# Expert network: the last 128 tokens through all eight experts, 21 tiles in place of 23, a first load of one tile

## The chip, the cores and the metric

One core of one Trainium2 chip runs the whole network. The metric is device time of one execution in microseconds (us), lower is better. TensorE (PE) does products, VectorE (DVE) and ScalarE (ACT) do elementwise work, GpSimd (POOL) issues the indirect DMAs, SyncE (SP) the other DMAs. Numbers are f32 unless said otherwise.

## The reference

Sixteen layers run in a row, each on a layer norm of the running `x`, with its result added to it. The two expert networks (stages L2f and L2g) are:

```python
x = x + _L2_ffn_ref(_layernorm(x, axis=-1), ...)
...
    HIDDEN = 128; FFN = 4 * HIDDEN; NUM_EXPERTS = 8; TOP_K = 2
    xt = x.reshape(b * s, h)
    probs = jax.nn.softmax(xt @ gate_w + gate_b, axis=-1)
    _, idx = jax.lax.top_k(probs, TOP_K)
    one_hot = jax.nn.one_hot(idx, NUM_EXPERTS, dtype=xt.dtype)
    mask = (one_hot.sum(axis=1) > 0).astype(xt.dtype)
    h1 = jax.nn.relu(jnp.einsum('th,ehf->etf', xt, w1) + b1[:, None, :])
    out_e = jnp.einsum('etf,efh->eth', h1, w2) + b2[:, None, :]
    out = jnp.einsum('eth,te->th', out_e, mask)
```

Each token counts the results of its two best experts, unweighted. An expert is 128 -> 512 -> 128.

## The kernel before, in words

A loop over two passes runs all sixteen stages on two samples (1024 tokens, channels on the partitions), so each expert stage runs twice: four times in all. Within a stage the five engines run their own hand-written instruction streams, and semaphores tie them; the order below is the order in which the code is written, and no scheduler moves it.

`expert_ffn` (L432) works in these steps:

1. SP issues 16 loads of 256 KB of expert weights into `wall` (L500, L501) while the layer norm and the gate product run. DVE finds each token's two experts; PE counts and ranks them (L526 to L530); DVE lays the experts' rows out in 23 tiles of 128 slots (an expert begins a new tile) and writes each row's slot (L671).
2. PE turns the tokens to rows (L521), ACT copies them twice to `tok` (L594), and POOL scatters them to the slots in DRAM: 8 tiles of tokens, two picks each, 16 indirect DMAs (L742). Beside it PE turns the picks (L535, L536) and lays the second bias down in two accumulating banks (L542).
3. Once all scatters have landed (`sent`), SP loads the slots back in groups of four tiles (L505). PE turns a group (`turn`, L549), ACT copies it to `xt` (`x_copy`, L605).
4. The loop over 23 tiles: ACT copies the tile's expert out of `wall` into one of three `wsel` buffers (`choose`, L611; the expert's number is loaded from a tile first), PE makes the hidden products (L559), DVE adds the bias and takes the relu (L707), PE makes the result (L568), DVE copies it (L719), POOL scatters it to `rows` (L747).
5. SP loads `rows` back (L509), DVE adds each token's two rows (L723), PE turns the sums and adds them to the bias banks (L584), DVE adds those to `xs` (L726).

Of the kernel before, what the change touches and what calls it, by code (L numbers as in the profile page):

```python
# [5 lines left out]
P = 128  # L6
# [8 lines left out]
E = 8  # L15
# [5 lines left out]
SLOTS = (2 * NB * T + E * (P - 1)) // P  # L21
# [410 lines left out]
def expert_ffn(g, name):  # L432
# [5 lines left out]
    GROUP = 4  # L438
    with Stage(g, name) as st:
# [14 lines left out]
        place = st.sb("place", [P, NT, E])  # L454
        taken = st.sb("taken", [P, 2, NT, E])
        slot_f = st.sb("slot_f", [P, 2 * NT])
        slot = st.sb("slot", [P, 2 * NT], U32)
# [9 lines left out]
        tok = st.sb("tok", [P, 2, NT, WIDE])  # L467
        xg = st.sb("xg", [P, SLOTS, WIDE])
        xt = st.sb("xt", [P, 2, GROUP, P])
# [14 lines left out]
        expert_in, sent, x_turned, x_in = (st.sem(n) for n in ("expert_in", "sent", "x_turned", "x_in"))  # L484
        groups = -(-SLOTS // GROUP)
# [5 lines left out]
        size = lambda k: min(GROUP, SLOTS - GROUP * k)  # L491
        gate = g.ps[:, 0, 0:NT * E].rearrange("p (t e) -> p t e", e=E)
        counts = g.ps[:, 2, 0:NT * E].rearrange("p (t e) -> p t e", e=E)
        ranks = g.ps[:, 1, 0:NT * E].rearrange("p (t e) -> p t e", e=E)
        with g.nc.Block() as block:  # L495
            @block.sync
            def _(sp):
                st.clear_spent(sp)
                for e in range(E):
                    sp.dma_start(wall[:, e, 0:FF], g.experts[0, :, e * FF:(e + 1) * FF]).then_inc(expert_in, 16)  # L500
                    sp.dma_start(wall[:, e, FF:2 * FF], g.experts[1, :, e * FF:(e + 1) * FF]).then_inc(expert_in, 16)  # L501
                sp.wait_ge(sent, 16 * 2 * NT)
                for k in range(groups):
                    a, z = GROUP * k * P, (GROUP * k + size(k)) * P
                    sp.dma_start(xg[:, GROUP * k:GROUP * k + size(k), :], g.slots[a:z, :].rearrange("(t p) w -> p t w", p=P)).then_inc(group_in[k], 16)  # L505
                sp.wait_ge(returned, 16 * SLOTS)
                for b in range(NB):
                    rows = g.rows[2 * b * T:2 * (b + 1) * T, :].rearrange("(t p k) c -> p t k c", p=P, k=2)
                    sp.dma_start(back[:, b * KT:(b + 1) * KT, :, :], rows).then_inc(back_in[b], 16)  # L509

            @block.tensor
            def _(pe):
# [13 lines left out]
                pe.matmul(g.ps[:, 2, 0:NT * E], g.cb[:, ONES:ONES + P], flat, start=True, stop=True).then_inc(counted, 1)  # L526
                pe.wait_ge(tri_ready, 1)
                pe.matmul(g.ps[:, 1, 0:NT * E], below[:, :], flat, start=True, stop=False)
                for j in range(1, NT):
                    mm = pe.matmul(g.ps[:, 1, j * E:NT * E], g.cb[:, ONES:ONES + P], flat[:, 0:(NT - j) * E], start=False, stop=(j == NT - 1))  # L530
                mm.then_inc(ranked, 1)
                for b in range(NB):
                    for t in range(b * KT, (b + 1) * KT):
                        at = (t - b * KT) * P
                        pe.matmul(g.ps[0:E, 4 + b, at:at + P], picks_of[:, 0, t, :], g.w("ident"), start=True, stop=False)  # L535
                        mm = pe.matmul(g.ps[0:E, 4 + b, at:at + P], picks_of[:, 1, t, :], g.w("ident"), start=False, stop=True)  # L536
                    mm.then_inc(mask_turned, 1)
                pe.wait_ge(b2_in, 1)
# [5 lines left out]
                def turn(k):  # L544
# [3 lines left out]
                    for j in range(size(k)):  # L548
                        mm = pe.transpose(g.ps[:, 4 + k % 2, j * P:(j + 1) * P], xg[:, GROUP * k + j, 0:P], g.w("ident"))  # L549
                    mm.then_inc(x_turned, 1)  # L550

                def hidden_products(n):
                    pe.wait_ge(chosen, n + 1)
                    if n % GROUP == 0:
                        pe.wait_ge(x_in, n // GROUP + 1)
                    if n >= 2:
                        pe.wait_ge(relu, n - 1)
                    for f in range(FT):
                        mm = pe.matmul(g.ps[:, n % 2, f * P:(f + 1) * P], wsel[:, n % 3, f * P:(f + 1) * P],  # L559
                                       xt[:, n // GROUP % 2, n % GROUP, :], start=True, stop=True)  # L560
# [13 lines left out]
                for n in range(SLOTS):  # L574
                    if n % GROUP == 0 and n // GROUP + 1 < groups:
                        turn(n // GROUP + 1)
# [3 lines left out]
                for b in range(NB):  # L580
                    for t in range(b * KT, (b + 1) * KT):
                        at = (t - b * KT) * P
                        pe.wait_ge(summed, t // 2 + 1)
# [4 lines left out]
            def _(act):  # L588
                ln.scalar(act)
                for b in range(NB):  # L590
                    act.wait_ge(tok_turned, b + 1)
                    act.wait_ge(cleared, 1)
                    for k in range(2):
                        act.activation(tok[:, k, b * KT:(b + 1) * KT, 0:P], g.ps[:, 6 + b, :].rearrange("p (t c) -> p t c", c=P), ACT.Copy).then_inc(tok_in, 1)  # L594
                act.wait_ge(b2_turned, 1)
                act.activation(b2_t[:, :], g.ps[0:E, 3, 0:P], ACT.Copy).then_inc(b2_in, 1)
                for b in range(NB):
                    act.wait_ge(mask_turned, b + 1)
                    act.activation(mask_t[:, b * KT:(b + 1) * KT, :], g.ps[0:E, 4 + b, :].rearrange("e (t c) -> e t c", c=P), ACT.Copy).then_inc(mask_in, 1)

                def x_copy(k):
                    act.wait_ge(x_turned, k + 1)
                    if k >= 2:
                        act.wait_ge(hidden, GROUP * (k - 1))
# [2387 lines left out]
```

## Time and profile before

| | us |
|---|---|
| median of 3 runs (lowest to highest) | 2908.37 (2906.75 to 2912.24) |
| the profiled execution: its own time | 2909.99 |
| its span | 2908.4 |
| PE busy (12494 products) | 2280.9 (78%) |
| DVE / ACT / POOL busy | 1790.6 / 1394.1 / 863.1 |

The granted TensorE clock was 0.912 of full speed over the span. A share of busy time is a mean over sixteen unlike stages, so what a stage's edit is worth has to be read from that stage's own stretch. Times in rows are from the span's start.

### The profile page before, as it was taken

The numbers are of one execution on the slowest core, as the hardware profiler recorded it, in microseconds if no ns is written. First come the engines' busy times: TensorE is split into PE (matmuls) and PEld (weight loads), VectorE is DVE, ScalarE is ACT, GpSimd is POOL, SyncE is SP. The second block draws the span as 40 slices with busy tenths as digits, with TensorE's granted clock in tenths as the row PEclk, the third lists the DMA queues.
The fourth block names the chain that finished last, engine by engine and source line by source line (L and its number), as shares of the span: only waits on it lengthen the run. The fifth ranks groups of instructions, "written<-read, shape, count | busy, mean of one in ns | idle before, by whom it ended". The sixth has DMA issues, their size and how long they took to land. (4 is left out here: it accounts for less than half of the span.)

```text
span 2908.4 us, 36691 instructions
## 1 busy us (share of the span) xinstructions
PE 2280.9 (78%) x12494; PEld 1080.1 (37%) x12494; DVE 1790.6 (62%) x3175; ACT 1394.1 (48%) x2320; POOL 863.1 (30%) x854
## 2 busy tenths in 40 slices
PE   6678879999866757777766788799998668576777
PEld 2231244544355236223222222445443542352232
DVE  5958475555545725985559495655556456259865
ACT  5534626555432434645455355265554325346454
POOL 2822141000235333742037211510002343327420
PEclk8997999999978878999989989899999788789999
DMA  3002000000032131000000020000000321300000
GB/s 143 0 6 77 13 1 9 1 1 1 0 104 62 56 100 34 0 1 1 11 5 0 22 62 12 1 9 1 1 1 1 105 66 52 102 33 0 1 1 15
DMA packets 58913, 80.93 MB, mean 28 GB/s; under 512 B 10784, under 2 KB 38944, under 8 KB 58464
## 3 DMA queue, kind: packets, MB, share of 16 engines
q1 hardware_dynamic: 49376, 63.81, 6.8%
q0 software_dynamic: 4992, 10.76, 1.1%
q10 hardware_dynamic: 4352, 3.94, 0.5%
q8 instruction: 103, 1.69, 0.2%
q14 instruction: 90, 0.74, 0.1%
HBM read 53.83 MB, written 26.08 MB: 27 GB/s over the span
## 5 line engine op out<-in xcount | busy, mean ns | idle before, releaser
L2269 ACT ACTIVATE L1b_pr<-ps,L1b_mneg 128x512 f32<-128x512 f32 x256 | 173.8, 683 | 190.9 <-DVE L1b_mneg L2310 190.9
L2308 DVE TENSOR_REDUCE L1b_m<-ps 128x2 f32<-128x1024 f32 x128 | 156.7, 1225 | 88.7 <-PE ps L2159 82.9
L96 ACT ACT_TABLE_LOAD x44 | 56.5, 1283 | 283.0 <-PEq L495 66.2
L1520 POOL TENSOR_TENSOR L0a_db<-L0a_du,L0a_bs 128x1024 f32<-128x1024 f32 x64 | 150.5, 2360 | 105.2 <-DVE L0a_du L1631 59.6
L1520 POOL TENSOR_TENSOR L3a_db<-L3a_du,L3a_bs 128x1024 f32<-128x1024 f32 x64 | 150.5, 2360 | 104.1 <-DVE L3a_du L1631 57.6
L1943 ACT ACTIVATE L0b_pt<-ps 128x1024 f32<-128x1024 f32 x128 | 125.6, 1023 | 97.8 <-PE ps L1843 97.7
L2031 DVE TENSOR_REDUCE L0b_mx<-ps 128x1 f32<-128x512 f32 x256 | 157.8, 682 | 20.9 <-PE ps L1830 18.2
L267 POOL CAST L1g_xc<-xn 128x512 bf16<-128x512 f32 x2 | 1.5, 732 | 558.9 <-DVE xn L142 558.9
L2334 DVE COPY L1b_prt<-ps 128x512 f32<-128x512 f32 x128 | 88.5, 691 | 126.5 <-PE ps L2172 126.2
L1648 DVE TENSOR_TENSOR_SCAN L3a_hs<-ps,L3a_db 128x1024 f32<-128x1024 f32 x64 | 146.0, 2281 | 5.4 <-ACT ps L1440 5.4
L1648 DVE TENSOR_TENSOR_SCAN L0a_hs<-ps,L0a_db 128x1024 f32<-128x1024 f32 x64 | 146.0, 2281 | 4.6 <-ACT ps L1440 4.6
L2159 PE MATMUL ps<-L1b_k,L1b_q 64*128 64x512 f32 x512 | 144.5, 641 | 0.0
L1943 ACT ACTIVATE L2b_pt<-ps 128x1024 f32<-128x1024 f32 (+3 forms) x128 | 85.3, 706 | 114.8 <-PE ps L1843 114.0
L2184 PE MATMUL ps<-L1b_prt,L1b_v 128*64 128x512 f32 x512 | 136.7, 614 | 4.1 <-issue 2.0
L2172 PE MATMUL ps<-weights,L1b_pr 128*128 128x128 f32 x1024 | 135.3, 274 | 0.0
L2028 DVE CUSTOM_DVE_ANT_0 L2b_unmasked<-ps,weights 128x128 bf16<-128x128 f32 (+3 forms) x256 | 110.7, 487 | 36.0 <-PE ps L1830 33.0
L2172 PEld LDWEIGHTS ps<-weights,L1b_pr 128*128 128x128 f32 x1024 | 115.8, 140 | 45.5 <-issue 43.5
L1327 PE MATMUL ps<-L3a_hc,weights 128*128 128x512 f32 x256 | 127.4, 625 | 5.1 <-ACT L3a_du L1420 3.0
L1327 PE MATMUL ps<-L0a_hc,weights 128*128 128x512 f32 x256 | 125.0, 615 | 5.1 <-ACT L0a_du L1420 3.0
L121 PE MATMUL ps<-xs,weights 128*128 128x512 f32 x128 | 79.5, 754 | 53.2 <-issue 10.8
L1830 PE MATMUL ps<-L0b_ks,L0b_qs 64*128 64x512 bf16 x256 | 91.3, 446 | 28.9 <-DMA L0b_ks<-stack_dram 17.0
L2755 DVE TENSOR_SCALAR L3b_re<-L3b_qb,L3b_zk 128x512 f32<-128x512 f32 x192 | 88.4, 534 | 23.0 <-ACT L3b_qb L2593 10.8
(697 smaller groups left out, 5267.4 us busy)
## 6 DMA issues: line engine op xcount, KB each, us to landing
L2f_wall<-expert_dram SPq DMA_DIRECT2D x32, 256.0 KB
L2g_wall<-expert_dram SPq DMA_DIRECT2D x32, 256.0 KB
weights<-w_dram SPq DMA_DIRECT2D x5, 941.5 KB, 13.7
L0b_qs<-stack_dram SPq DMA_DIRECT2D x32, 96.0 KB, 2.2
stack_dram<-L0b_cut SPq DMA_DIRECT2D x24, 128.0 KB, 2.1
L2b_qs<-stack_dram SPq DMA_DIRECT2D x32, 96.0 KB, 2.3
stack_dram<-L2b_cut SPq DMA_DIRECT2D x24, 128.0 KB, 2.1
L2f_xg<-slots SPq DMA_DIRECT2D x10, 288.0 KB, 4.8
```

The source lines that it names most:

```text
L1327: mm = pe.matmul(g.ps[:, SUM + k, :], g.w("ident"), hc[:, n % DEEP, k, :], start=(s == 0), stop=(s == NS - 1))
L1520: pool.tensor_tensor(db[:, n % DEEP, :, :], du[:, b, :, :], bcast(bs[:, n % DEEP, :], 1, 2), ALU.mult).then_inc(input_ready, 1)
L1648: dve.tensor_tensor_scan(flat(hs), decay_banks(n).rearrange("p k t -> p (k t)"), flat(db), 0.0, ALU.mult, ALU.add).then_inc(scanned, 1)
L1830: pe.matmul(g.ps[:, bank, 0:span(t)], qs[r:r + HALF, b, 2 * i + c, t * P:(t + 1) * P], ks[r:r + HALF, b, 2 * i + c, 0:span(t)], start=True ...
L1943: act.activation(pt[:, n % 3, 2 * half:2 * half + 2, q0:T], g.ps[:, 2 * (s % 2):2 * (s % 2) + 2, q0:T], ACT.Exp).then_inc(prob, 1)
L2028: dve.tensor_tensor_reduce(unmasked[:, e % 3, 0:span(t)], g.ps[:, bank, 0:span(t)], g.w("causal_row", T - span(t)), 1.0, -3e38, ALU.add, A ...
L2031: dve.tensor_reduce(mx[:, u, col:col + 1], g.ps[:, bank, 0:T], AX.X, ALU.max).then_inc(top_in, 1)
L2159: mm = pe.matmul(g.ps[:, 2 * (s % 2) + h, :], q[HE * h:HE * h + HE, u % 3, t * P:(t + 1) * P], k[HE * h:HE * h + HE, u % 3, :], start=True ...
L2172: mm = pe.transpose(g.ps[:, 4 + h, j * P:(j + 1) * P], pr[:, s % 2, h, j * P:(j + 1) * P], g.w("ident"))
L2184: mm = pe.matmul(g.ps[HE * h:HE * h + HE, PV, :], v[:, u % 4, j, HE * h:HE * h + HE], prt[:, u % 2, h, j, :], start=(j == 0), stop=(j == K ...
L2269: act.activation(pr[:, s % 2, h, :], g.ps[:, 2 * (s % 2) + h, :], ACT.Exp, bias=mneg[:, s % 2, h:h + 1], accum_out=total[:, u % 2, t, h:h ...
L2308: dve.tensor_reduce(m[:, s % 2, :], g.ps[:, 2 * (s % 2):2 * (s % 2) + 2, :], AX.X, ALU.max).then_inc(max_raw, 1)
```

## The change

One tile of tokens, the last 128 of the second sample (`SENT = 7`), is no longer scattered. It goes through all eight experts straight from `xn` and `wall`: `full_hidden_products` and `full_results` on PE, `full_relus` on ACT, and on DVE a sum over the experts with the token's picks (`keep`) as factors, into the place that its turned sum takes (`both[:, SENT]`). The others need at most 21 tiles of slots. Groups of linear loads are 1, 2, 3, 4, 4, 4 and 3 tiles. The picks are turned after the eight experts; the weight loads have a semaphore each; ACT's `x_copy` of a group stands ahead of the `choose` beside it. Cut to its core (the wait on `full_sum` is in `turn`, the relus and the loop of copies are ACT's, and the last piece is DVE's, after its plan and ahead of its loop):

```diff
-SLOTS = (2 * NB * T + E * (P - 1)) // P
+SLOTS = (2 * (NB * T - P) + E * (P - 1)) // P
...
-    GROUP = 4
+    SENT = NT - 1
+    GROUPS = (1, 2, 3, 4, 4, 4, 3)
...
-                sp.wait_ge(sent, 16 * 2 * NT)
+                sp.wait_ge(sent, 16 * 2 * SENT)
...
                 mm.then_inc(gate_ready, 1)
-                for b in range(NB):
-                    for t in range(KT):
-                        mm = pe.transpose(g.ps[:, 6 + b, t * P:(t + 1) * P], g.xn[:, b, t * P:(t + 1) * P], g.w("ident"))
-                    mm.then_inc(tok_turned, 1)
-                pe.transpose(g.ps[0:E, 3, 0:P], g.w("e2_b2"), g.w("ident")).then_inc(b2_turned, 1)
+                pe.transpose(g.ps[0:E, 1, 0:P], g.w("e2_b2"), g.w("ident")).then_inc(b2_turned, 1)
+                for t in range(SENT):
...
+                def full_hidden_products(e):
+                    pe.wait_ge(expert_in[e], 32)
+                    if e >= 2:
+                        pe.wait_ge(full_relu, e - 1)
+                    for f in range(FT):
+                        mm = pe.matmul(g.ps[:, 2 + e % 2, f * P:(f + 1) * P], wall[:, e, f * P:(f + 1) * P], g.xn[:, 1, T - P:T], start=True, stop=True)
+                    mm.then_inc(full_hidden, 1)
+
+                def full_results(e):
+                    pe.wait_ge(full_relu, e + 1)
+                    for f in range(FT):
+                        mm = pe.matmul(g.ps[:, 4 + e // 4, e % 4 * P:(e % 4 + 1) * P], hd[:, e % 2, f, :], wall[:, e, FF + f * P:FF + (f + 1) * P],
+                                       start=(f == 0), stop=(f == FT - 1))
+                    mm.then_inc(full_out, 1)
+
+                full_hidden_products(0)
                 pe.wait_ge(mask_ready, 1)
...
                 mm.then_inc(ranked, 1)
+                for e in range(E):
+                    if e + 1 < E:
+                        full_hidden_products(e + 1)
+                    full_results(e)
+                pe.wait_ge(slots_ready, 1)
...
+                    else:
+                        pe.wait_ge(full_sum, E)
...
+                def full_relus(e):
+                    act.wait_ge(full_hidden, e + 1)
+                    if e >= 2:
+                        act.wait_ge(full_out, e - 1)
+                    if e == 0:
+                        act.wait_ge(ids, 2)
+                    for f in range(FT):
+                        ins = act.activation(hd[:, e % 2, f, :], g.ps[:, 2 + e % 2, f * P:(f + 1) * P], ACT.Relu, bias=wall[:, e, 2 * FF + f:2 * FF + f + 1])
+                    ins.then_inc(full_relu, 1)
+
+                take_tokens(0)
+                full_relus(0)
+                take_tokens(1)
+                for e in range(1, E):
+                    full_relus(e)
...
                 for n in range(SLOTS):
+                    if n == first_of[group_of[n]] and group_of[n] + 1 < groups:
+                        x_copy(group_of[n] + 1)
                     if n + 2 < SLOTS:
                         choose(n + 2)
-                    if n % GROUP == 0 and n // GROUP + 1 < groups:
-                        x_copy(n // GROUP + 1)
...
+                for e in range(E):
+                    dve.wait_ge(full_out, 4 * (e // 4) + 4)
+                    at = g.ps[:, 4 + e // 4, e % 4 * P:(e % 4 + 1) * P]
+                    if e == 0:
+                        dve.tensor_scalar(both[:, SENT, :], at, keep[:, 0:1], None, ALU.mult).then_inc(full_sum, 1)
+                    else:
+                        dve.wait_ge(full_sum, e)
+                        dve.scalar_tensor_tensor(out=both[:, SENT, :], in0=at, scalar=keep[:, e:e + 1], in1=both[:, SENT, :],
+                                                 op0=ALU.mult, op1=ALU.add).then_inc(full_sum, 1)
```

On PE, at the gate product of L2f, the order before; `L2f_mask` is the count of the picks:

```order
L517 MATMUL ps<-weights,xn 128x8 x8
L521 MATMUL ps<-weights,xn 128x128 x8
L523 MATMUL ps<-weights 8x128
L526 MATMUL ps<-L2f_mask,cb 128x64
L528 MATMUL ps<-L2f_mask,L2f_below 128x64
```

Now the first expert's hidden products stand ahead of the count:

```order
L525 MATMUL ps<-weights,xn 128x8 x8
L527 MATMUL ps<-weights 8x128
L530 MATMUL ps<-weights,xn 128x128 x7
L539 MATMUL ps<-xn,L2f_wall 128x128 x4
L552 MATMUL ps<-L2f_mask,cb 128x56
L555 MATMUL ps<-L2f_mask,L2f_below 128x56
```

The count waits behind four products that weren't there. On PE, from the bias product (L542, now L573) to the first results of the loop, before:

```order
L542 MATMUL ps<-L2f_mask_t,L2f_b_t 128x512 x2
L549 MATMUL ps<-weights,L2f_xg 128x128 x4
L559 MATMUL ps<-L2f_xt,L2f_wsel 128x128 x4
L549 MATMUL ps<-weights,L2f_xg 128x128 x4
L559 MATMUL ps<-L2f_xt,L2f_wsel 128x128 x4
L568 MATMUL ps<-L2f_wsel,L2f_h 128x128 x4
```

The same place now:

```order
L573 MATMUL ps<-L2f_mask_t,L2f_b_t 128x512 x2
L582 MATMUL ps<-weights,L2f_xg 128x128
L593 MATMUL ps<-L2f_xt,L2f_wsel 128x128 x4
L582 MATMUL ps<-weights,L2f_xg 128x128 x2
L593 MATMUL ps<-L2f_xt,L2f_wsel 128x128 x4
L602 MATMUL ps<-L2f_wsel,L2f_h 128x128 x4
```

One turned tile stands ahead of the first products, and the second products now belong to the group turned just ahead of them. On ACT, at the opening of the loop (the third choice of an expert), before:

```order
L605 ACTIVATE L2f_xt<-ps 128x512
L610 TENSOR_LOAD L2f_expert_of
L610 ISA x2
L611 ISA
L611 ACTIVATE L2f_wsel<-L2f_wall 128x1028
L605 ACTIVATE L2f_xt<-ps 128x512
```

The same place now:

```order
L657 ACTIVATE L2f_xt<-ps 128x128
L657 ACTIVATE L2f_xt<-ps 128x256
L662 TENSOR_LOAD L2f_expert_of
L662 ISA x2
L663 ISA
L663 ACTIVATE L2f_wsel<-L2f_wall 128x1028
L657 ACTIVATE L2f_xt<-ps 128x384
```

Each group's copy has moved ahead of the choice that it stood behind.

## Rows read from the trace of the kernel before

**Rows 1.** Windows: the first L2f in two stretches, then both passes of L2g.

```profile
core 0: us, PE busy (x) PEld busy (x) DVE busy (x) ACT busy (x) POOL busy (x), PEclk, DMA share, GB/s
826.31:847.84 21.53, 5.12 (x23) 2.69 (x21) 1.84 (x9) 3.18 (x4) 15.60 (x16) 0.58 0.17 56
852.85:900.17 47.32, 46.66 (x387) 45.21 (x387) 31.65 (x125) 24.59 (x26) 20.73 (x22) 0.97 0.14 43
1036.70:1139.54 102.84, 69.70 (x485) 60.41 (x485) 43.89 (x169) 35.66 (x43) 38.33 (x44) 0.78 0.29 95
...
2487.56:2590.00 102.44, 69.52 (x485) 60.36 (x485) 43.56 (x169) 35.66 (x43) 38.34 (x44) 0.78 0.29 95
```

**Rows 2.** Timeline of L2f, scatters to first products: start, length, engine, line, idle before.

```profile
827.82 0.96 POOL L742 DMA_INDIRECT slots<-L2f_tok,L2f_slot  x1 [0.31 <-issue]
...
845.52 0.96 POOL L742 DMA_INDIRECT slots<-L2f_tok,L2f_slot  x1 [0.30 <-issue]
847.84 3.34 SPq L505 DMA_DIRECT2D L2f_xg<-slots  x6
...
850.95 1.12 PE L549 MATMUL ps<-weights,L2f_xg 128*128 128x128 f32 x4 [19.52 <-DMA L2f_xg<-slots]
...
852.10 0.60 ACT L605 ACTIVATE L2f_xt<-ps 128x512 f32<-128x512 f32 x1 [19.28 <-PE ps L549]
852.74 1.06 ACT L611 ACTIVATE L2f_wsel<-L2f_wall 128x1028 f32 x1
...
852.85 2.04 PE L559 MATMUL ps<-L2f_xt,L2f_wsel 128*128 128x128 f32 x8 [0.78 <-ACT L2f_xt L605]
```

**Rows 3.** Timeline of the loop of L2f, from one group's turn to the next.

```profile
863.10 0.60 PE L549 MATMUL ps<-weights,L2f_xg 128*128 128x128 f32 x4
...
863.93 1.06 ACT L611 ACTIVATE L2f_wsel<-L2f_wall 128x1028 f32 x1 [0.73 <-PE ps L568]
864.43 1.06 PE L568 MATMUL ps<-L2f_wsel,L2f_h 128*128 128x128 f32 x8
...
865.33 1.06 PE L559 MATMUL ps<-L2f_xt,L2f_wsel 128*128 128x128 f32 x8
...
870.95 0.60 PE L549 MATMUL ps<-weights,L2f_xg 128*128 128x128 f32 x4
```

**Rows 4.** DMA issues: size of one in KB, median us from issue to landing.

```profile
L0b_qs<-stack_dram SPq DMA_DIRECT2D x32, 96.0 KB, 2.2
```

**Rows 5.** Timeline of L2f: PE around the count, the turned picks and the bias.

```profile
821.09 0.42 PE L523 MATMUL ps<-weights 128*8 128x128 f32 x1
...
822.90 0.24 PE L526 MATMUL ps<-L2f_mask,cb 128*128 128x64 bf16 x1 [1.40 <-DVE L2f_mask L650]
...
828.93 0.38 PE L535 MATMUL ps<-weights,L2f_picks_of 128*8 128x128 f32 x2
...
829.14 0.38 PE L536 MATMUL ps<-weights,L2f_picks_of 128*8 128x128 f32 x2
...
829.46 1.98 PE L542 MATMUL ps<-L2f_mask_t,L2f_b_t 8*128 8x512 f32 x4
```

**Rows 6.** Windows of half a microsecond around the changes of the granted clock.

```profile
828.50:829.00 0.50, 0.50 (x6) 0.39 (x5) 0.00 (x0) 0.00 (x0) 0.28 (x1) 0.94 0.00 0
...
832.00:832.50 0.50, 0.00 (x0) 0.00 (x0) 0.00 (x0) 0.50 (x1) 0.50 (x1) 0.50 0.07 19
...
1058.50:1059.00 0.50, 0.00 (x0) 0.00 (x0) 0.00 (x0) 0.00 (x0) 0.20 (x2) 1.00 0.00 0
...
855.50:856.00 0.50, 0.50 (x5) 0.50 (x4) 0.50 (x3) 0.22 (x1) 0.00 (x0) 0.64 0.04 12
```

**Rows 7.** Lines L861 and L881: copies and sums out of PSUM, min/median/max in ns.

```profile
L861 ACT ACTIVATE L2a_prt<-ps x16: 277/438/599, 794.8 to 2261.0; 128x128 f32<-128x128 f32 x4, 128x256 f32<-128x256 f32 x4, 128x384 f32<-128x384 f32 x4, 128x512 f32<-128x512 f32 x4
...
L881 DVE SCALAR_TENSOR_TENSOR L2a_none<-ps,L2a_later x16: 283/482/692, 790.7 to 2258.1; 128x128 f32<-128x128 f32 x4, 128x256 f32<-128x256 f32 x4, 128x384 f32<-128x384 f32 x4, 128x512 f32<-128x512 f32 x4
```

**Rows 8.** Timeline of L2f's end: the sums of the rows loaded back.

```profile
909.34 0.76 DVE L723 TENSOR_TENSOR L2f_both<-L2f_back 128x256 f32<-128x256 f32 x2 [0.61 <-DMA L2f_back<-rows]
```

More of the change, by code:

```diff
@@ L437, in expert_ffn @@
     NT = NB * KT
-    GROUP = 4
+    SENT = NT - 1
+    GROUPS = (1, 2, 3, 4, 4, 4, 3)
+    first_of = [sum(GROUPS[:k]) for k in range(len(GROUPS) + 1)]
+    group_of = [k for k in range(len(GROUPS)) for _ in range(GROUPS[k])]
     with Stage(g, name) as st:
@@ L453, in expert_ffn @@
         limit = st.sb("limit", [P, E])
[L454 to L457, printed above, removed]
+        place = st.sb("place", [P, SENT, E])
+        taken = st.sb("taken", [P, 2, SENT, E])
+        slot_f = st.sb("slot_f", [P, 2 * SENT])
+        slot = st.sb("slot", [P, 2 * SENT], U32)
+        keep = st.sb("keep", [P, E])
+        hd = st.sb("hd", [P, 2, FT, P])
         past = st.sb("past", [P, SLOTS, E])
@@ L529, in _ @@
-                for j in range(1, NT):
-                    mm = pe.matmul(g.ps[:, 1, j * E:NT * E], g.cb[:, ONES:ONES + P], flat[:, 0:(NT - j) * E], start=False, stop=(j == NT - 1))
+                pe.wait_ge(b2_in, 1)
+                pe.matmul(g.ps[:, 1, 0:SENT * E], below[:, :], flat[:, 0:SENT * E], start=True, stop=False)
+                for j in range(1, SENT):
+                    mm = pe.matmul(g.ps[:, 1, j * E:SENT * E], g.cb[:, ONES:ONES + P], flat[:, 0:(SENT - j) * E], start=False, stop=(j == SENT - 1))
@@ L547, in turn @@
                         pe.wait_ge(x_in, k - 1)
-                    for j in range(size(k)):
-                        mm = pe.transpose(g.ps[:, 4 + k % 2, j * P:(j + 1) * P], xg[:, GROUP * k + j, 0:P], g.w("ident"))
+                    else:
+                        pe.wait_ge(full_sum, E)
+                    for j in range(GROUPS[k]):
+                        mm = pe.transpose(g.ps[:, 4 + k % 2, j * P:(j + 1) * P], xg[:, first_of[k] + j, 0:P], g.w("ident"))
                     mm.then_inc(x_turned, 1)
@@ L574, in _ @@
                 for n in range(SLOTS):
[L575 to L576 removed]
+                    if n == first_of[group_of[n]] and group_of[n] + 1 < groups:
+                        turn(group_of[n] + 1)
                     if n + 1 < SLOTS:
@@ L650, in _ @@
                 dve.tensor_tensor(mask[:, :, :], picks_of[:, 0, :, :], picks_of[:, 1, :, :], ALU.add).then_inc(mask_ready, 1)
+                dve.tensor_tensor(keep[:, :], picks_of[:, 0, SENT, :], picks_of[:, 1, SENT, :], ALU.add).then_inc(keep_ready, 1)
                 dve.wait_ge(counted, 1)
@@ L713, in _ @@
                 for n in range(SLOTS):
-                    if n % GROUP == 1 and n // GROUP + 1 < groups:
-                        rows_of(n // GROUP + 1)
+                    if n + 1 == first_of[group_of[n] + 1] and group_of[n] + 1 < groups:
+                        rows_of(group_of[n] + 1)
                     if n + 1 < SLOTS:
@@ L721, in _ @@
                     dve.wait_ge(back_in[b], 16)
-                    for t in range(b * KT, (b + 1) * KT, 2):
-                        dve.tensor_tensor(both[:, t:t + 2, :], back[:, t:t + 2, 0, :], back[:, t:t + 2, 1, :], ALU.add).then_inc(summed, 1)
+                    for t in range(b * KT, min(SENT, (b + 1) * KT), 2):
+                        z = min(SENT, t + 2)
+                        dve.tensor_tensor(both[:, t:z, :], back[:, t:z, 0, :], back[:, t:z, 1, :], ALU.add).then_inc(summed, 1)
                 for b in range(NB):
```

92 lines of the change are left out of this document (49 added, 43 removed).

## The prediction

> **What bounds the kernel now.** I read first how much time the edited stage holds. An L2g takes 102.8 and 102.4 us in the two passes, and the L2f's look the same, so four such stages hold some 410 of the 2908 us [rows 1]. Nothing outside them is edited. Then I read the first L2f by stretches. From 826.31 to 847.84 POOL is the only busy engine worth the name (15.60 of 21.53 us, PE 5.12): the stage waits for 16 scatters, issued one after the other. From 852.85 to 900.17 PE is busy 46.66 of 47.32 us: the loop over 23 tiles is bound by PE [rows 1]. The timeline shows the seam between the two: the last scatter is issued at 845.52, the first linear load at 847.84, its data lets PE start at 850.95 after 19.52 us of idling, and the first products start at 852.85, once four tiles are turned and copied [rows 2]. All of this is serial, so what leaves it leaves the stage. The idle PE in the scatters' stretch is the room into which the change puts the eight experts.
>
> **The change, term by term, for one stage.** Negative is time saved.
>
> A. Two scatters go. From 827.82 to 845.52 lie 14 pitches, 1.264 us each [rows 2]; two are -2.53.
>
> B. The first load holds 72 KB (128 rows of 144 numbers) and not 288. The trace has no load of this size on this path. The old one takes 850.95 - 847.84 = 3.11 us [rows 2], which is the upper end (no gain); the nearest small one, 96 KB, lands in 2.2 [rows 4]. Ends 0 and -0.9; I take -0.8, since the size is nearer to the small row.
>
> C. One tile is turned and copied ahead of the first products. Now that takes 852.85 - 850.95 = 1.90 [rows 2]. One of four transposes is 1.12/4 = 0.28, a copy of 128x128 out of PSUM 0.28 [rows 7], and the two gaps seen between turn, copy and products are 0.03 and 0.15 [rows 2]: 0.74, so -1.15.
>
> D. Two tiles of the loop go. A group of four, its turn included, takes 870.95 - 863.10 = 7.85, so 1.96 a tile [rows 3]: -3.92.
>
> E. The second tile's products now need the copy of the group turned just ahead of them, where they used to run from the first group. PE idles for the drain of the transposes, the copy of two tiles (0.28 for one, 0.44 as the median of one to four tiles [rows 7]) and the gap of 0.15: +0.75. Between 0.6 and 0.9.
>
> F. The copy stands ahead of the choice beside it. In rows 3 the choice starts at 863.93 and the products that need it at 865.33. If the copy goes first it starts at 863.74, after the turn, takes 0.60 [rows 2], and the choice (1.06) ends near 865.45 to 865.55, some 0.1 to 0.25 late. The load of the expert's number does not add to this: behind a copy that had not waited for the loop, the choice followed at 852.74, 0.04 after the copy's end [rows 2]. Six openings, minus what the same move gives back (choice n+3 is then no longer late): +0.5, between 0 and 1.5.
>
> G. TensorE's clock. PE starts at half rate after its idle time, and the row in which the rate rises is 855.50 to 856.00 (0.64 granted), 4.7 us after the first transpose [rows 2, 6]. If PE idles again before the loop, this repeats; but less of it is spent on turn and copy (0.9 instead of 1.9 us), so about 1 us more of products runs at half: +0.5.
>
> H. The count of the picks waits behind the first expert's hidden products. PE is free at 821.51 and the count starts at 822.90 after 1.40 idle [rows 5]. Eight passes at half rate take 2 x 0.90 = 1.8 (the pitch of a set of eight at full rate is 865.33 - 864.43 = 0.90 [rows 3]), less one transpose that is gone, so the scatters start about 0.2 later in L2f; in L2g the clock is still up there and it fits. Mean +0.1, between 0 and 0.5.
>
> I. The second load of returned rows is a quarter smaller, and its last sum half as long; DVE waits 0.61 us for it [rows 8]: -0.3.
>
> The slots' arithmetic on DVE gets a few columns narrower and `keep` fits in DVE's wait for the count: 0. Thirteen more semaphores are cleared by SP at the start of the next stage, ahead of any DMA that is due: 0.
>
> Sum: -2.53 - 0.8 - 1.15 - 3.92 + 0.75 + 0.5 + 0.5 + 0.1 - 0.3 = -6.85. Four stages: -27.4.
>
> **What has to stay hidden.** The added work costs nothing only if PE and ACT are done when the first tile lands, at 850.95 - 2.53 - 0.8 = 847.6. PE has the counts behind it at about 823.5. Then follow 15 sets of eight passes (7 hidden, 8 results), 0.90 each at full rate, 1.8 at half. In the trace of before, PE starts again at 822.90 and has the full rate at 828.50 to 829.00 (0.94) [rows 5, 6]. Taken so, 2.8 sets run by 828.5 and the other 12.2 end at 839.5. The 16 products that turn the picks come 0.21 apart (828.93, 829.14 [rows 5]): 842.9. Bias products 1.98: 844.9. ACT needs four relus an expert, near 0.28 each [rows 7], 1.1 us against PE's 1.8, so PE sets the pace; ACT's second copy of the picks ends at 843.6 and its first two choices at 846.2. DVE's eight sums at about 0.3 [rows 7] end by 842. So PE has 2.7 us to spare and ACT 1.4. The group turned at the start finds both.
>
> **A rule on the clock.** What the rows show is mixed. PE's idle time after the bias products brought the clock to 0.50 by 832.00 in L2f, while in L2g it was still 1.00 in the window 1058.50 to 1059.00 with PE idle [rows 6]. The Trainium skill (TensorE: Matmul & The Clock Gate, "HAM oscillation — how this bites in real kernels") says that waits for a DMA that are long enough throttle PE, so that each burst opens cold, while shorter ones leave it warm. By that rule the loop could open at full rate in this kernel. I make of it the first rival; what it would give is worked out from rows alone.
>
> **Rivals.**
>
> 1. The clock stays up into the loop. PE would idle 844.9 to 847.6, 2.7 us, where it idled 19.52. Then the 3.8 us of products at half rate (4.7 less 0.9) shrink to half and the first transpose too: -2.0 more, -8.85 a stage, 2909.99 - 35.4 = 2874.6. For it speaks the window at 1058.50; against it the one at 832.00.
>
> 2. The loads and openings give less. The first load lands no sooner (B = 0) and each of six openings costs 0.25 (F = 1.5): -5.05 a stage, 2889.8. For it: the six loads go out within 3.34 us and share the engines; the small row is of another transfer. Against: a first load has nothing ahead of it in its queue.
>
> 3. The eight experts outlast the scatters, on the other side. If the clock does not rise during them, the 12.2 sets take 11.0 more and the turned picks 3.4 more, and PE is done at 859.3, 11.7 after the first tile. The stage ends 11.7 - 6.85 = 4.9 later than before: 2909.99 + 19.4 = 2929. It decides from 2.7 us on, that is when three more sets run at half rate, or when an expert's four relus take over 2.1 us. Against it: before, PE reached the full rate with less to do in the same place, and held it through the loop with the same sets of eight (0.97 granted over 852.85 to 900.17 [rows 1]).
>
> **How the numbers follow.** The profiled execution took 2909.99, 1.6 above the median of 2908.37 and inside the three runs' spread, so I take the sum against it: 2909.99 - 27.4 = 2882.6. Chances: forecast 0.60, with its own range 2877 to 2888; rival 1 0.18 (in some of the four stages it would lie between the two); rival 2 0.13; rival 3 0.09, a part of it only slightly late and near no change. The range 2871 to 2895 holds the first three with some margin and leaves out rival 3. A measurement of this kernel tells about 0.2% (5.8 us) from no change: faster by more 0.89, within it 0.02, slower 0.09.
>
> **What would show it.** Right: 14 scatters at 1.26 and 21 at the end; first linear load 2.3 us after its issue; PE in sets of eight from about 823 on, the clock at full rate by 829, the bias products over before the first transpose; the first products near 848.3 on the old scale; groups of four at 7.9 to 8.1 us. Wrong: a first transpose whose wait ends with the bias products or DVE's sum (rival 3); a PE clock of 1.00 in the first microseconds of the loop (rival 1); waits for `wsel` over 0.25 at each opening, or 3 us for the small load (rival 2). If the scatters' pitch grew beside a busy PE, ACT and DVE, term A would be wrong, since this pitch was seen beside idle engines only.

## The result, and the profile after

The changed kernel takes 2927.86 us in the median of five runs (2926.85 to 2942.85), the one before 2908.37 (2905.77 to 2912.24): ratio 1.0073, 95% interval 1.0058 to 1.0089. It is slower, where 2882.6 was forecast.

The profiled execution of after is the slowest of its five: 2942.85 us, span 2941.2. So I compare the edited stages, from the count of the picks to the last sum. The windows of both L2g stages, from there (columns: length, busy time and instructions of PE, PEld, DVE, ACT, POOL, granted clock, DMA share, GB/s):

```profile
1054.23:1150.30 96.07, 75.43 (x537) 69.88 (x537) 39.68 (x155) 35.40 (x61) 33.65 (x35) 0.84 0.21 67
2524.98:2618.08 93.10, 71.48 (x537) 66.14 (x537) 39.69 (x155) 34.94 (x59) 33.57 (x35) 0.86 0.22 69
```

Before, the same stretches take 90.41 (1049.13 to 1139.54, the end as in [rows 1]) and 90.45. Over all four stages after is 17.1 us longer; the other 15.7 of the 32.8 between the two spans lie in stages that nothing edited. That unedited rest takes 2546 us in the profiled execution of before, 2562 in that of after, and 2535 to 2564 over the profiled executions of all kernels here. The medians are 19.5 apart. Below are the means of the four stages, in us, with those of the experiments that follow. A stage is cut at the first product of the count of the picks, the first transpose of a loaded tile, the first products of the loop, the loop's last result and the last sum into `xs`:

| kernel | count to first transpose | to first products | to last result | to last sum | stage |
|---|---|---|---|---|---|
| before | 27.73 | 1.87 | 48.22 | 12.68 | 90.5 |
| after | 34.86 | 1.21 | 46.38 | 12.33 | 94.8 |
| no experts | 24.02 | 0.90 | 46.82 | 12.25 | 84.0 |
| groups only | 26.63 | 0.91 | 51.25 | 12.40 | 91.2 |
| all scatters paced | 30.92 | 0.91 | 47.00 | 12.21 | 91.0 |
| eight paced | 27.79 | 0.91 | 47.18 | 12.27 | 88.2 |
| scatters held | 36.49 | 0.90 | 47.34 | 12.34 | 97.1 |
| split | 27.83 | 0.89 | 46.87 | 11.96 | 87.6 |
| split, no sum wait | 26.70 | 0.91 | 47.24 | 11.97 | 86.8 |
| split, choice first | 27.29 | 0.91 | 46.00 | 11.97 | 86.2 |
| choice first, picks last | 26.47 | 0.90 | 46.06 | 11.97 | 85.4 |
| choice first, L2g paced | 25.46 | 0.90 | 46.13 | 11.97 | 84.5 |

All that after loses, it loses between the count and the first transpose. There the timeline of its first L2f has, on POOL and SP, what was forecast: scatters 1.26 apart, two fewer of them, and the loads behind them (against [rows 2]):

```profile
842.51 0.96 POOL L805 DMA_INDIRECT slots<-L2f_tok,L2f_slot  x1 [0.30 <-issue]
843.78 0.96 POOL L805 DMA_INDIRECT slots<-L2f_tok,L2f_slot  x1 [0.30 <-issue]
845.05 0.96 POOL L805 DMA_INDIRECT slots<-L2f_tok,L2f_slot  x1 [0.30 <-issue]
847.35 3.50 SPq L512 DMA_DIRECT2D L2f_xg<-slots  x7
```

The first tile's load has a median of 1.9 us to landing, so it lands near 849.3. But PE isn't ready. Its sets of eight in the same stretch (L539 hidden products, L545 results):

```profile
831.37 1.06 PE L539 MATMUL ps<-xn,L2f_wall 128*128 128x128 f32 x8
832.27 1.06 PE L545 MATMUL ps<-L2f_wall,L2f_hd 128*128 128x128 f32 x8
833.16 1.06 PE L539 MATMUL ps<-xn,L2f_wall 128*128 128x128 f32 x8
835.38 1.16 PE L545 MATMUL ps<-L2f_wall,L2f_hd 128*128 128x128 f32 x8 [1.16 <-issue]
836.38 1.06 PE L539 MATMUL ps<-xn,L2f_wall 128*128 128x128 f32 x8
844.02 2.08 PE L545 MATMUL ps<-L2f_wall,L2f_hd 128*128 128x128 f32 x8 [6.59 <-ACT L2f_hd L641]
845.89 1.62 PE L539 MATMUL ps<-xn,L2f_wall 128*128 128x128 f32 x8
849.83 3.21 PE L545 MATMUL ps<-L2f_wall,L2f_hd 128*128 128x128 f32 x16 [2.31 <-ACT L2f_hd L641]
...
856.99 1.98 PE L573 MATMUL ps<-L2f_mask_t,L2f_b_t 8*128 8x512 f32 x4
858.90 0.34 PE L582 MATMUL ps<-weights,L2f_xg 128*128 128x128 f32 x1
```

And ScalarE's relus between them:

```profile
828.89 1.14 ACT L641 ACTIVATE L2f_hd<-ps,L2f_wall 128x128 f32<-128x128 f32 x4 [0.65 <-PE ps L539]
830.68 1.14 ACT L641 ACTIVATE L2f_hd<-ps,L2f_wall 128x128 f32<-128x128 f32 x4 [0.65 <-PE ps L539]
834.19 1.14 ACT L641 ACTIVATE L2f_hd<-ps,L2f_wall 128x128 f32<-128x128 f32 x4 [2.36 <-remote]
842.83 1.14 ACT L641 ACTIVATE L2f_hd<-ps,L2f_wall 128x128 f32<-128x128 f32 x4 [7.50 <-remote]
848.63 2.17 ACT L641 ACTIVATE L2f_hd<-ps,L2f_wall 128x128 f32<-128x128 f32 x8 [4.67 <-PE ps L539]
```

To the fourth relu all is as reckoned: sets 0.90 apart, a relu every 1.79. The next ones start long after the products that they need. The relu of 842.83 needs the set that starts at 833.16 and is done by 834.2, and a buffer that the results of 832.27 had read; ACT was free at 835.33. It waits 7.5 us, and the trace can name no instruction that ended it: `remote` stands where a signal comes so long after every instruction that could have sent it that none is named. The first of the two experts at 848.63 needs a set that ended at 837.44 (836.38 and 1.06). ACT's own signals are prompt: PE's results start at 844.02, 0.05 after the relus end. So what is late is TensorE's signal to another engine. The packed trace has the signals' own times, and they say it outright: those of the eight sets of hidden products come 0.01, 0.01, 0.01, 0.01, 1.73, 8.59, 11.18 and 1.28 us after the sets' modelled ends. Some arrive while scatters are still issued (834.16, 842.80), others together some 2.6 us after the last one (848.5 to 848.8). In the list of waits nothing of `remote` stood in the kernel before; now (total us, times, longest):

```profile
ACT L2g_hd L641 <- remote: 25.6, 4, 10.3
DVE L2g_both L751 <- remote: 23.5, 2, 15.3
ACT L2f_hd L641 <- remote: 21.5, 3, 11.6
```

The length of a wait is not the delay. DVE's 15.3 us began while the results that it needs were still being made; they ended at 1064.20, 10.6 us before it starts:

```profile
1063.04 1.16 PE L545 MATMUL ps<-L2g_wall,L2g_hd 128*128 128x128 f32 x8
1074.84 0.35 DVE L751 TENSOR_SCALAR L2g_both<-ps,L2g_keep 128x128 f32<-128x128 f32 x1 [15.30 <-remote]
```

The longest delay of a signal in after is 13.9 us (second pass of L2f: a set's end at 2298.71, its signal at 2312.61).

The Trainium skill (Perfetto Trace Analysis, "Tensor Engine Instruction (MATMUL, LD_WEIGHTS)") warns of this gap: a matmul's end in the trace is computed, while the semaphore goes out once PSUM has acknowledged the data and becomes visible later still. The rows agree that a signal can come after the end shown, and put the gap at up to 13.9 us, where the Trainium skill gives no size. They don't tell which of its steps took the time.

### The profile page after: what moved, and what is told of

Same layout as the page of the kernel before. It is cut to its first block and busy times, and to the rows that moved or that the text cites. A ratio compares the mean times of both kernels' runs of the same rounds, so it can differ in the third digit from the quotient of the medians.

```text
span 2941.2 us, 37607 instructions
## 1 busy us (share of the span) xinstructions
PE 2346.3 (80%) x12842; PEld 1141.0 (39%) x12862; DVE 1790.7 (61%) x3179; ACT 1421.7 (48%) x2444; POOL 847.0 (29%) x838
## 5 line engine op out<-in xcount | busy, mean ns | idle before, releaser
L2006 ACT ACTIVATE L0b_pt<-ps 128x1024 f32<-128x1024 f32 x128 | 125.6, 1023 | 97.1 <-PE ps L1906 97.0
L1390 PE MATMUL ps<-L3a_hc,weights 128*128 128x512 f32 x256 | 123.3, 608 | 5.1 <-ACT L3a_du L1483 3.0
L1390 PE MATMUL ps<-L0a_hc,weights 128*128 128x512 f32 x256 | 122.6, 605 | 5.1 <-ACT L0a_du L1483 3.0
L121 PE MATMUL ps<-xs,weights 128*128 128x512 f32 x128 | 81.8, 773 | 52.5 <-issue 10.1
```

What stands on the lines that cost most here:

```text
L1390: mm = pe.matmul(g.ps[:, SUM + k, :], g.w("ident"), hc[:, n % DEEP, k, :], start=(s == 0), stop=(s == NS - 1))
L2006: act.activation(pt[:, n % 3, 2 * half:2 * half + 2, q0:T], g.ps[:, 2 * (s % 2):2 * (s % 2) + 2, q0:T], ACT.Exp).then_inc(prob, 1)
```

## Experiments

The edits are shown cut to their core. There were two theories at the start. S: TensorE's signals reach the other engines late while GpSimd issues scatters back to back. R: the experts' own chain is slower than I reckoned, scatters or not.

**No experts.** From after, the experts' products, relus and sums are left out (the last tile gets zeros):

```diff
-                full_hidden_products(0)
-                for e in range(E): ...            # PE, ACT and DVE alike
+                dve.tensor_scalar(both[:, SENT, :], g.w("ident"), 0.0, None, ALU.mult)
```

> This leaves the last tile's way through the experts out: no products, relus and sums of it (zeros stand for its result), all else as in the changed kernel (14 scatters, 21 tiles, groups of 1, 2, 3, 4, 4, 4, 3). Theory S (TensorE's signals reach the other engines late while GpSimd issues scatters back to back, which holds up the eight experts) and theory R (the eight experts' own work is slower than I had it) both expect what my terms A to I gave without the experts: 2878 to 2888 us. If the time is over 2895, the saving of 27 us was wrong in itself, and the experts are the smaller part of the miss.

2888.86 us (2885.83 to 2891.04), ratio to before 0.9935 (0.9915 to 0.9955). The median lies 0.9 us above my range. The stages lose 6.5 us each against -6.95, which is my sum without H (this kernel has no hidden products ahead of the count): the terms hold, and what is wrong is the cover.

**Scatters held.** From after:

```diff
                 pool.wait_ge(slots_ready, 1)
+                pool.wait_ge(full_out, E)
```

> GpSimd starts the 14 scatters only when all eight experts' results are there. Theory S: with no scatter beside them the signals are prompt, a set of eight passes takes 0.9 us and the eight experts end about 12 to 14 us after the counts (at 838 to 840 in the first L2f); the scatters come after, and the whole is within 10 us of the changed kernel (2925 to 2940). Theory R: the experts keep their pace of the changed kernel (end at 853), the scatters come on top, +15 us a stage: 2980 to 2990.

2953.24 us, ratio 1.0158 (1.0134 to 1.0182), between the ranges, but the trace decides. With no scatter beside them the last relus stand

```profile
834.90 1.14 ACT L641 ACTIVATE L2f_hd<-ps,L2f_wall 128x128 f32<-128x128 f32 x4 [0.64 <-PE ps L539]
836.69 1.14 ACT L641 ACTIVATE L2f_hd<-ps,L2f_wall 128x128 f32<-128x128 f32 x4 [0.64 <-PE ps L539]
838.48 1.14 ACT L641 ACTIVATE L2f_hd<-ps,L2f_wall 128x128 f32<-128x128 f32 x4 [0.64 <-PE ps L539]
```

1.79 apart to the end, and every signal of the experts' products comes within 0.02 us. R falls: the sets that follow the count begin at 825.99 and the last ends at 840.8, 14.8 us, near the 12 to 14 that I had reckoned.

**Split.** From after, four experts early with the picks turned between them, four behind the loop, in its tail:

```diff
+    EARLY = 4
+                full_hidden_products(1); turn_picks(0); full_results(0); turn_picks(1)
+                ... experts 2, 3          # early
+                for e in range(EARLY, E): ... # behind the loop
```

> Four experts are computed at the start of the scatters, with the picks turned between them, and four after the last tile of the loop, while the rows are written and loaded back; the sums likewise. Theory S: the first four signals are nearly prompt, as in the changed kernel, later ones have 10 us of slack, and no row of scatters stands beside the last four: 2878 to 2892 us. Theory R: four experts at the end take 2.5 us or more each, as in the changed kernel, and the end of the stage moves by 3 to 6 us: 2895 to 2912.

2891.54 us (2886.42 to 2906.91), ratio 0.9955 (0.9934 to 0.9976): both kernels are beaten. Four experts hide behind the loop (12.0 us from last result to last sum, with none 12.25). Early ones still meet late signals (up to 12.3 us late, in L2g), and the first turn waits for their sums.

**One transpose a round.** Before, with 16 rounds beside the scatters: a transpose, a signal, ScalarE's copy, a signal back.

```diff
+                for r in range(PINGS):
+                    if r: pe.wait_ge(pong, r)
+                    pe.transpose(g.ps[:, 2, ...], g.xn[:, 1, T - P:T], g.w("ident")).then_inc(ping, 1)
```

> The kernel before, with 16 rounds of one transpose on TensorE and one copy of 128x128 on ScalarE, each waiting for the other, beside the scatters behind the bias products; nothing of the experts' work and no big load on any engine. Theory S: the rounds take 0.65 us at first, then some take over 2 us, the 16 rounds end only about when the scatters end (846 or later in the first L2f), and the loop starts later than before: 2910 to 2930 us. Theory R, and a theory that ScalarE's instructions come late only in the long run of relus: 16 rounds of 0.6 to 0.7 us, done by 843, time as before (2908).

2907.38 us, ratio 0.9996 (0.9981 to 1.0011), rounds of 0.70 and, at half clock, 0.84 us; none late:

```profile
831.37 0.28 ACT L613 ACTIVATE L2f_bounce<-ps 128x128 f32<-128x128 f32 x1 [1.58 <-PE ps L551]
...
843.28 0.28 ACT L613 ACTIVATE L2f_bounce<-ps 128x128 f32<-128x128 f32 x1 [0.56 <-PE ps L551]
```

S falls in its simple form: beside one transpose a round the scatters delay nothing. The new theory S2: they do so beside a dense TensorE.

**Four kinds of dense rounds.** Before, with 16 rounds in two banks, none with the experts' data, each kernel executed once:

```diff
+                    if r >= 2: pe.wait_ge(pong, r - 1)
+                    for f in range(4):   # dense; two: 2 products of 256; wide: 1 of 512; short: 4 of 32
+                        mm = pe.matmul(g.ps[:, 2 + r % 2, ...], g.xn[:, 0, ...], g.xn[:, 1, ...])
+                    mm.then_inc(ping, 1)
```

> The kernel before, with 16 rounds beside the scatters in which TensorE works nearly all the time: each round is one set as an expert's (four products 128x128, 0.90 us at full rate), then a signal, and ScalarE's copy of 128x512 out of that bank, two banks in turn. Theory S2 (a dense TensorE beside back-to-back scatters has its signals delivered late): from the third or fourth scatter on, copies start 1 us or more after their set has ended, with waits put down to `remote` or to PE far behind its end, a few of 4 to 10 us; the 16 rounds take over 20 us instead of 15, and the run 2910 to 2940. Rival W (what is late comes from the experts' own operands or from ScalarE's four small relus): copies follow their sets within 0.3 us as in the rounds of one transpose, 16 rounds take 14.5 to 18 us, and the run 2905 to 2912.

> As the dense rounds, but each round is a single product of 512 columns instead of four of 128: the same columns and the same busy time, a quarter of TensorE's instructions and weight loads. If the number of TensorE's instructions beside the scatters is what delays its signals (S2, by count): copies follow their products within 0.3 us and the rounds take 0.9 to 1.2 us each, 2905 to 2912. If it is TensorE's busy time (S2, by share): late copies as in the dense rounds. By rival W: nothing late here either.

> The dense rounds with two products of 256 columns a round: the same columns and busy time as four of 128 and one of 512, TensorE instructions between the two (4.4 matmuls a us, against 8.9 and 2.2). S2 by count, with a limit between: late signals that are fewer or start later than in the dense rounds (16 rounds in 16 to 22 us, 2907 to 2935), or none if the limit lies above 4.4. If it were weight loads or busy time alone there would be no such step.

> The dense rounds with four products of 32 columns a round: as many TensorE instructions as an expert's set, but a quarter of the columns, so that ScalarE's copy (0.60 us) sets the pace and TensorE is busy less than two thirds of the time. S2 by count: late signals as in the dense rounds (waits of 2 us and more, 16 rounds over 18 us, 2925 to 2960). S2 by busy time: rounds of 0.6 to 0.9 us, none late, 2905 to 2912.

| round | matmul records per us | us of the run | longest waits of ACT in the first L2f, us |
|---|---|---|---|
| 1 product of 512 | 2.2 | 2907.71 | one of 1.95, the last; the others 0.26 and 0.36 |
| 2 of 256 | 4.4 | 2937.65 | 1.2 to 2.9 from the sixth copy to the tenth |
| 4 of 128 | 8.9 | 2960.18 | 2.2 to 5.0, from the third copy to the sixth |
| 4 of 32 | 8.3 | 2977.75 | 3.7 to 5.1, from the fourth to the sixth |

A product of the rounds leaves two records. The last three runs came out above their expected ranges, by 3 to 20 us. The wide rounds aren't free of it either: in each of the other three stages two to four of the last copies wait longer, up to 2.2 us. The wide and the dense rounds, timelines of ACT in the middle of the scatters:

```profile
835.68 0.60 ACT L614 ACTIVATE L2f_bounce<-ps 128x512 f32<-128x512 f32 x1 [0.36 <-PE ps L551]
836.54 0.60 ACT L614 ACTIVATE L2f_bounce<-ps 128x512 f32<-128x512 f32 x1 [0.26 <-PE ps L551]
```

```profile
841.86 0.60 ACT L615 ACTIVATE L2f_bounce<-ps 128x512 f32<-128x512 f32 x1 [2.27 <-PE ps L552]
847.48 0.60 ACT L615 ACTIVATE L2f_bounce<-ps 128x512 f32<-128x512 f32 x1 [5.02 <-remote]
```

And the short ones:

```profile
839.36 0.60 ACT L615 ACTIVATE L2f_bounce<-ps 128x512 f32<-128x512 f32 x1 [3.65 <-remote]
845.04 0.60 ACT L615 ACTIVATE L2f_bounce<-ps 128x512 f32<-128x512 f32 x1 [5.08 <-remote]
```

How busy TensorE was shows in windows, first of the wide rounds, then of the short ones before their first late signal (columns as above):

```profile
830.00:844.00 14.00, 13.76 (x31) 4.37 (x29) 0.00 (x0) 8.96 (x15) 10.64 (x12) 1.00 0.18 58
```

```profile
831.00:835.00 4.00, 3.87 (x33) 3.65 (x32) 0.00 (x0) 1.19 (x2) 3.09 (x4) 0.97 0.16 55
```

The wide rounds are busy 13.76 of 14.00 us with 31 matmul records, all at full clock, and prompt to the last round. The short ones have 33 in 4 us. I had expected them to leave TensorE idle a third of the time; they don't (3.87 of 4.00), so what they show is only that a quarter of the columns helps nothing. What delays the signals is then mainly the number of TensorE's instructions (matmuls with a weight load each, which these rounds don't tell apart), and not its busy time (wide), nor the number of signals (one a round in all four), nor the experts' operands. Part of the longer runs is no delay: the rounds outlast the scatters, and the short ones then take 1.71 us each, at half clock.

**All scatters paced.** From after:

```diff
+                            pool.memset(pause[:, :], 0.0).then_inc(paused, 1)
+                            pool.wait_ge(paused, 2 * t + k + 1)
                             pool.indirect_dma_start(g.slots[:, :], ...)
```

> The changed kernel, with a memset of 128x512 on GpSimd ahead of each of the 14 scatters, so that their pitch grows from 1.26 us to some 1.9 to 2.2. S2: at the loop's pitch (1.96) TensorE's signals are prompt, so the experts' relus come every 1.8 us and no wait is put down to `remote`; the scatters end some 10 to 13 us later, the first transpose waits for the load, and the stage from count to first transpose takes 33 to 37 us instead of 34.9: 2925 to 2950. Rival (it is scatters at any pitch): relus late as before, first transpose after DVE's sum; over 2955.

2913.41 us (2911.2 to 2923.2), ratio 1.0020 (1.0005 to 1.0035). Scatters stand 1.78 apart, no wait is `remote`, the recorded signals of the experts' products are within 0.02 us of their ends, and the relus are back:

```profile
834.82 0.97 POOL L808 DMA_INDIRECT slots<-L2f_tok,L2f_slot  x1 [0.28 <-POOL L2f_pause L806]
836.60 0.97 POOL L808 DMA_INDIRECT slots<-L2f_tok,L2f_slot  x1 [0.28 <-POOL L2f_pause L806]
```


```profile
836.80 1.14 ACT L642 ACTIVATE L2f_hd<-ps,L2f_wall 128x128 f32<-128x128 f32 x4 [0.65 <-PE ps L540]
838.59 1.14 ACT L642 ACTIVATE L2f_hd<-ps,L2f_wall 128x128 f32<-128x128 f32 x4 [0.65 <-PE ps L540]
```

I had expected 2925 to 2950: the price was smaller, as the memset adds 0.52 a scatter and not 0.7 to 0.9. With 14 x 0.52 us thrown away the kernel is still faster than after.

**Eight paced.** The same, with `if 2 * t + k < 8:` ahead of the memset.

> The changed kernel with a memset ahead of the first eight scatters only (the stretch in which the experts run), the other six back to back. If late signals need both, instructions of TensorE in a dense row and scatters back to back: relus every 1.8 us, the first transpose 28.0 us after the count (31.1 in the kernel with all 14 paced, less six times 0.52), 87.9 a stage: 2896 to 2904, faster than before. If a few scatters back to back anywhere delay what comes after (the turned picks, the bias products): the first transpose at 30 us or later, 2905 to 2920.

2904.9 us (2896.51 to 2914.22), ratio 0.9987 (0.9974 to 1.0001), 88.2 a stage. The turned picks and bias products beside the last six scatters are prompt; the first transpose waits for its load again, 27.8 after the count. By the stages it should be 4 x 2.3 = 9 faster than before; the medians are 2 apart, and 0.9 above my range. The unedited rest is 5 us longer here than before in the profiled executions; I have no other cause.

**Split, no sum wait; choice first; picks last; L2g paced.** The split, with early results in banks that the turns don't use and all sums behind the loop; then each with one edit more:

```diff
-                        pe.wait_ge(full_sum, EARLY)
+                        pe.wait_ge(full_relu, EARLY)
@@ choice first
+                    if n == 0: x_copy(1)
+                    if n + 2 < SLOTS: choose(n + 2)
+                    if n > 0 and n == first_of[group_of[n]] ...: x_copy(group_of[n] + 1)
@@ on that, picks last: turn_picks(0), turn_picks(1) behind full_results(3)
@@ on choice first, L2g paced
+                            if name == "L2g" and 2 * t + k < 5: pool.memset(...)
```

> Four experts beside the start of the scatters and four behind the loop, as in the split kernel, but the first turn waits for no sum: the early results lie in banks that the turns do not use, and all eight sums stand behind the loop on VectorE. Expected: count to first transpose 24.0 to 25 us in all four stages (split: 25.5 in L2f, 30.2 in L2g), behind the loop no more than 1 us over the 12.0 of the kernel without experts: 2880 to 2892. If ScalarE's relus of the third and fourth expert still wait for late signals past the first load (choice and copy queued behind them): L2g 2 to 4 us more each, 2886 to 2898.

> As the split without a sum wait, with one edit: from the second tile on ScalarE's choice of the weights stands ahead of the copy of the next group again, as in the kernel before (the first copy stays ahead, since the second tile needs it). My term F took +0.5 us a stage for the copy standing first. If that holds, 2 us less than the split without a sum wait: 2886 to 2891 where that measured 2890.8. Rival: the openings already show no wait over 0.16 us in the kernel without experts, so within 1 us of the same time.

> As the split with the choice first, but the 16 products that turn the picks (32 TensorE instructions) stand behind the four early experts instead of between them, so that the experts' rounds end by the fourth or fifth scatter. If the number of TensorE's instructions since the scatters began decides: the relus of L2g no longer wait for late signals (8.8 us now), count to first transpose falls there from 30.2 to 25 to 28, while the copies of the picks come late with the scatters' end in all stages, +0 to 1.5 each: 2878 to 2888. If it is the scatters' time alone that decides, L2g stays at 30 and the run at 2884 to 2890.

> The split with the choice first, and in L2g alone, where the late signals are left, a memset ahead of the first five scatters. Expected there: no wait of ScalarE for remote signals, five times 0.52 more for the scatters, count to first transpose 26.6 instead of 30.2, so 3 us less in two stages: 2878 to 2886. If the pace does nothing for these: 2.6 us more in two stages, 2887 to 2894.

Measured: 2890.78 (0.9932, 0.9910 to 0.9953), 2884.49 (0.9925, 0.9903 to 0.9946), 2887.31 (0.9937, 0.9916 to 0.9958) and 2883.38 (0.9916, 0.9894 to 0.9937). Their intervals overlap; the stages tell more. No sum wait: I had expected 24 to 25 us from count to first transpose in all four stages; L2f has 24.1 and 24.0, but L2g 28.6 and 30.1, with ScalarE's relus still late. Choice first: 47.24 to 46.00 us in the loop, and a median 1.5 below the range expected. Picks last: the relus of L2g are prompt, count to first transpose falls there from 30.2 to 25.95 and 27.7, and rises in L2f from 24.4 to 26.1, since now the copies of the picks are late (waits up to 12.4 us there). By its stages it is 0.8 us shorter than choice first, though its median is not. So the TensorE instructions issued since the scatters began push what follows. L2g paced: 30.2 to 26.5, no `remote` there.

**Groups only.** Before, with tiles in groups of 1, 2, 3, 4, 4, 4, 4, 1 and the copy ahead of the choice:

```diff
-    GROUP = 4
+    GROUPS = (1, 2, 3, 4, 4, 4, 4, 1)
```

> The kernel before with one part of the change alone: 23 tiles in groups of 1, 2, 3, 4, 4, 4, 4, 1 (the first linear load holds one tile, copy ahead of choice), all 16 scatters, no experts of the last 128 tokens. By my terms B, C, E, F and G, with 0.1 for one more opening: -0.1 a stage, so 2906 to 2909. By the trace of the kernel without experts (load 1.2 sooner, turn and copy 1.0 shorter, openings of 0.1 each, products at half rate for as long): -1.5 a stage, 2901 to 2905.

2917.23 us (2903.21 to 2926.09, 12 runs), ratio 1.0026 (1.0011 to 1.0041): both guesses missed. Load and turn give 2.1 us a stage, and the loop takes 3.0 more.

## Why the prediction was wrong

**The sum of the terms held.** The kernel without experts has them all: A is -2.53 (pitch 1.26). B is -1.2, more than the -0.8 taken and outside its ends (0 and -0.9): 1.89 us from issue to transpose. Together 27.73 to 24.02 is -3.71, forecast -3.33. H lies ahead of the count, and in before and after alike the count starts 0.06 us behind DVE's mask: near 0, as taken. C is -0.97, forecast -1.15. D to G come to -1.40, forecast -2.17: the copy ahead of the choice (F) costs more than 0.5. The rows of the split without and with the choice first, turns of groups of four:

```profile
867.67 0.60 PE L601 MATMUL ps<-weights,L2f_xg 128*128 128x128 f32 x4
875.77 0.60 PE L601 MATMUL ps<-weights,L2f_xg 128*128 128x128 f32 x4
```

```profile
863.42 0.60 PE L601 MATMUL ps<-weights,L2f_xg 128*128 128x128 f32 x4
871.26 0.60 PE L601 MATMUL ps<-weights,L2f_xg 128*128 128x128 f32 x4
```

8.10 a group and 7.84, the latter as before [rows 3]: F is 1.2 a stage, inside its bounds. G costs more too, and my row was an exception. Before, the first L2f has the full rate 3 us after its first products [rows 6], but the other three stages 5.9 to 6.0 us after them (first L2g: products at 1078.54, full rate from 1084.56), 5.2 in the mean. Without experts it takes 5.9 to 7.3, 6.9 in the mean. The 1.7 us more at half rate are some 0.85 lost, where 0.5 was taken. The windows around the change of the clock, in the first L2g of before and in the first L2f without experts (its first products start at 846.35):

```profile
1084.00:1084.50 0.50, 0.50 (x5) 0.50 (x4) 0.31 (x2) 0.00 (x0) 0.00 (x0) 0.50 0.00 0
1084.50:1085.00 0.50, 0.50 (x6) 0.50 (x6) 0.19 (x1) 0.00 (x0) 0.00 (x0) 0.94 0.00 0
```

```profile
851.50:852.00 0.50, 0.50 (x4) 0.50 (x4) 0.50 (x3) 0.00 (x0) 0.00 (x0) 0.50 0.00 0
852.00:852.50 0.50, 0.50 (x6) 0.50 (x5) 0.50 (x3) 0.00 (x0) 0.00 (x0) 0.77 0.00 0
```

I is -0.43 (-0.3). Sum -6.5 a stage.

**The step that failed is "What has to stay hidden".** It took 15 sets at 0.90 and let each wait last as long as its producer, so that "PE has 2.7 us to spare". PE did its sets at 0.90 and had the full clock (1.00 from 833 to 834), but in after's L2f they end at 853.0. Forecast were 839.5 on the old clock of the span, 841.3 on this one (count at 825.02, not 823.2). Of these 11.7 us PE idles 10.1 in its three waits for relus that TensorE's late signals held up (1.16, 6.59 and 2.31); the other 1.6 are sets at half rate, since the clock fell while PE stood. The first transpose comes at 858.90, 9.5 us after its tile. In the mean of the four stages the experts cost 10.8 a stage over the kernel without experts (94.8 against 84.0), and 4 x 10.8 - 4 x 6.5 = +17, against +19.5 between the medians.

**The rivals.** Rival 3 named place, size (11.7 us late, 2929) and sign, with a chance of 0.09, but not the cause: half rate. That its 2929 meets the measured 2927.86 is luck, since it was worked out from another mechanism. The clock rose as forecast; it fell to 0.50 only once PE stood waiting (0.50 from 842 to 843). What would show it wrong was named rightly: a first transpose that waits for bias products or sums. I asked whether the scatters' pitch would suffer beside a busy PE, and not whether PE would suffer beside the scatters. The trace of before couldn't tell: in its scatters' stretch no one waits for TensorE after 829.5, and in its loop, as dense, scatters stand 1.96 apart.

## What to carry to other kernels

Idle time of an engine is not free room: before moving a chain of short round trips into it, look in the trace for a place where the same two streams have already run side by side at that rate, and if there is none, bound the cost upward by the whole length of the chain. Beside back-to-back indirect DMAs give TensorE few, wide instructions, or put the work in the tail, where four experts cost nothing here. When a wait is put down to `remote`, compare the end of the producer with the start of the waiter before believing either, and don't take the length of the wait for the delay.

## What the runs showed of the hardware

- TensorE's signals were up to 13.9 us late beside scatters 1.26 us apart, at 8.9 matmul records a us; none was at 1.78 apart (all scatters paced). At 1.26 apart, 2.2 records a us made only one to four of the last of 16 rounds late, 4.4 most from the sixth on, and one transpose a round none. If both load one thing in proportion, a scatter of 128 rows weighs over 4.5 / (1/1.264 - 1/1.78) = 20 matmul records: an estimate from these runs, which leaves out whatever buffer lets the first signals pass.
- ScalarE's and VectorE's signals stayed prompt meanwhile (the recorded ones in after within 0.02 us of an end of theirs), and the scatters kept their pitch (1.26).
- What is shared stays open. Every execution here is recorded, each instruction is meant to leave a record, so the recording itself may be what fills up. The Trainium skill (NOTIFIC — the notification-queue block, "Overflow: three behaviours, one of which stalls the engine") says that the block's inner pipeline holds a producer back rather than lose a record. That fits a delay that goes by the number of instructions and not by busy time. The trace does lose records in this stretch, but whether signals are late or not: it holds 7, 10, 9 and 7 of the wide rounds' 16 signals in the four stages, and 11, 4, 8 and 7 of the 16 of the prompt single transposes. That neither shows nor rules out that the recording holds TensorE back. No run here shows what fills up, nor what an unrecorded execution would take, so the cause of the late signals stays open, and with it whether the advice above holds without a recording.
